# Router logits of an AdaLN attention and mixture-of-LoRA block computed with the router's weights held in the array, then transposed back

## What is computed

```python
h = layernorm(x) * (1 + ca) + sa
x = x + ga * attention(h)                      # causal, one head of 256, layer norm and residual inside
h = layernorm(x) * (1 + cb) + sb
x = x + gb * ffn(h)

def ffn(x):                                    # x flattened to rows of 256
    gate, up = x @ Wg.T, x @ Wu.T              # 704 hidden columns
    base = silu(gate) * up @ Wd.T
    probs = softmax(x @ Wr.T)                  # the router: 8 experts
    topw, topi = top_k(probs, 2)               # two experts for each row
    expert_w = sum(one_hot(topi, 8) * topw)
    for e in range(8):                         # LoRA of rank 16 for each expert
        g = x @ Ag[e].T @ Bg[e].T * 2;  u = x @ Au[e].T @ Bu[e].T * 2
        h = silu(gate + g) * (up + u)
        acc += (h @ Ad[e].T @ Bd[e].T * 2) * expert_w[:, e]
    return base + acc
```

## Time and profile before

| | |
|---|---|
| median of 3 runs | 670.26 us (670.22 to 670.79) |
| the profiled execution | 669.96 us, of which the span from first to last instruction is 668.1 us |
| granted TensorE clock, mean | 0.997 of full speed |
| PE busy | 652.1 us, 98% of the span, 3890 matmuls |
| DVE, ACT, POOL busy | 466.5, 360.3 and 369.5 us |
| DMA queue of the data | 6.6% of 16 engines' span |

### The profile page before, as it was taken

The page is one execution under the profiler, slowest core; times in us unless marked ns, Lnnn a source line. Parts: engine busy times, 40 slices in busy tenths (PEclk is TensorE's granted clock), DMA queues, the critical chain, the costliest instruction groups (busy, mean ns, idle before and its releaser), DMA issues.

```text
span 668.1 us, 10913 instructions
## 1 busy us (share of the span) xinstructions
PE 652.1 (98%) x3890; PEld 561.4 (84%) x3890; DVE 466.5 (70%) x1146; ACT 360.3 (54%) x646; POOL 369.5 (55%) x442
## 2 busy tenths in 40 slices
PE   8799999999999999999999999999999999999996
PEld 6488987888889987888889897887889998798885
DVE  5857676888785776688776677689886757547323
ACT  1766466545555547555455446564455456654543
POOL 1099366538658236657676317665666525633644
PEclk9999999999999999999999999999999999999999
DMA  8400020000000020000000001000000000000000
GB/s 308 138 1 1 2 64 0 1 1 32 0 1 32 1 65 1 0 1 33 0 1 32 1 6 59 1 1 33 1 0 27 7 1 1 1 1 1 32 0 33
DMA packets 15032, 15.47 MB, mean 23 GB/s; under 512 B 1793, under 2 KB 13697, under 8 KB 14977
## 3 DMA queue, kind: packets, MB, share of 16 engines
q1 hardware_dynamic: 14976, 14.76, 6.6%
HBM read 10.57 MB, written 4.19 MB: 22 GB/s over the span
## 4 chain that ended last, share of the span: by engine, by line
PE 84%; DVE 10%; ACT 3%; issue 1%; DMA 1%; POOL 0%; SPq 0%; DVEq 0%; ACTq 0%
PE ps L1265 78%; PE ps L1274 6%; DVE hid L1112 2%; DVE rstd L844 1%; DVE zb L864 1%; DMA xs<-in_L_attn_x 1%; DVE neg_mean L1176 1%; ACT xr L587 1%; ACT act_s L725 1%; DVE zb L867 0%; DVE stat L998 0%; DVE stat L861 0%; DVE topi L1057 0%; DVE xr L1007 0%; DVE nr_a L842 0%
## 5 line engine op out<-in xcount | busy, mean ns | idle before, releaser
L475 POOL TENSOR_TENSOR ring_lo<-hid,ring_hi 128x512 fp32r<-128x512 f32 x144 | 187.2, 1304 | 110.0 <-ACT ring_hi L733 109.4
L725 ACT ACTIVATE act_s<-ps 128x512 f32<-128x512 f32 x120 | 71.6, 597 | 123.0 <-PE ps L1265 122.4
L1112 DVE TENSOR_TENSOR hid<-act_s,ps 128x512 f32<-128x512 f32 x120 | 82.1, 684 | 78.9 <-ACT act_s L725 74.1
L733 ACT ACTIVATE ring_hi<-hid 128x512 fp32r<-128x512 f32 (+1 forms) x144 | 90.4, 627 | 5.3 <-PE ps L1265 3.5
L1265 PE MATMUL ps<-wdT_hi,ring_hi 128*128 128x256 f32 x192 | 53.2, 283 | 0.0
L1265 PE MATMUL ps<-wdT_lo,ring_hi 128*128 128x256 f32 x192 | 52.7, 280 | 0.0
L467 POOL TENSOR_TENSOR xT_lo<-tr_full,xT_hi 128x512 fp32r<-128x512 f32 x28 | 35.9, 1297 | 29.0 <-ACT xT_hi L597 29.0
L1265 PE MATMUL ps<-wdT_hi,ring_lo 128*128 128x256 f32 x160 | 44.7, 280 | 0.0
L1265 PE MATMUL ps<-vv_hi,pT_hi 128*128 128x256 f32 x144 | 42.9, 298 | 0.1
L1265 PE MATMUL ps<-tm_hi,bgT_hi 128*128 128x512 f32 x96 | 39.5, 411 | 2.4 <-DVE hid L1112 2.4
L482 POOL TENSOR_TENSOR xr<-xr,y_gb 128x256 f32<-128x256 f32 x31 | 22.6, 754 | 33.6 <-DVE y_gb L1147 33.6
(11 more groups left out here) (232 smaller groups left out, 2018.2 us busy)
## 6 DMA issues: line engine op xcount, KB each, us to landing
out<-xr SPq DMA_DIRECT2D x7, 512.0 KB, 2.9
xs<-in_L_attn_x SPq DMA_DIRECT2D x3, 1024.0 KB, 5.7
xs<-in_L_attn_x SPq DMA_DIRECT2D x2, 512.0 KB, 4.7
s_mod<-in_L_wmod SPq DMA_DIRECT2D x2, 512.0 KB, 7.6
s_qkvT<-in_L_attn_qkv SPq DMA_DIRECT2D x1, 768.0 KB, 7.4
wgT_raw<-in_L_ffn_Wg SPq DMA_DIRECT2D x1, 704.0 KB, 7.9
wuT_raw<-in_L_ffn_Wu SPq DMA_DIRECT2D x1, 640.0 KB, 8.7
wdT_raw<-in_L_ffn_Wd SPq DMA_DIRECT2D x1, 640.0 KB, 5.7
```

The lines of the kernel that those rows point to most:

```text
L475: pool.tensor_sub(ring[1][:, place(n), :], hid[:, n % HID, :], ring[0][:, place(n), :].bitcast(fp32)).then_inc(h_lo.sem, 1)
L725: nc.scalar.activation(act_s[:, n % 2, :], ps[:, 2 * (n % 2), :], ACT.Silu).then_inc(silu_ready.sem, 1)
L733: nc.scalar.activation(ring[0][p0:P, place(n), :], hid[p0:P, n % HID, :], ACT.Copy).then_inc(h_hi.sem, 1)
L1112: V.tensor_mul(hid[:, n % HID, :], act_s[:, n % 2, :], ps[:, 2 * (n % 2) + 1, :]).then_inc(h_ready.sem, 1)
```

## The change

`logits(ci)` is split in two. `logits_across(ci)` holds the router's weights in the array (16 or 8 columns) and moves all 512 rows of x past them: 2 k x 2 = 4 matmuls; the logits come out turned, 16 partitions by 512. A new DVE instruction, `logits_copy(ci)`, copies them out of PSUM into `logit_rows`, a view of 16 partitions of the tile `y_gb`. `logits_back(ci)` on PE waits for the copy and turns them back with 4 transposes, into the places where the logits stood before. DVE's `router_shift` waits for these. Two semaphores are new.

In half 0, `logits_across(0)` stands where `logits(0)` stood, and `logits_back(0)` behind the second piece of `probs_values`. In half 1, `logits_back(1)` stands one base product later, and `FILL` moves two `down`s behind the next `adapters`. On DVE, `router_shift(1)` moves behind the statistics of that step, and the moments and the guess of the next batch's first norm behind `hidden(13)`; POOL's three Newton steps for it come one unit later.

```diff
+        logit_rows = y_gb[0:2 * E, :, :].rearrange("p t d -> p (t d)")
...
-                            if not last and 13 <= r < 13 + NEWTON:
-                                newton(b, LN1_X, 0, NT, r - 13)
+                            if not last and 14 <= r < 14 + NEWTON:
+                                newton(b, LN1_X, 0, NT, r - 14)
...
+                def logits_copy(ci):
+                    dve.wait_ge(logits_wide.sem, logits_wide.at(b, ci))
+                    if ci == 0:
+                        dve.wait_ge(out_ready.sem, out_ready.at(b, -1))
+                    V.tensor_copy(logit_rows, ps[0:2 * E, LOGIT_BANK[ci], :]).then_inc(logits_copied.sem, 1)
...
+                logits_copy(0)
                 router_shift(0)
...
                     if r == 12:
-                        router_shift(1)
+                        logits_copy(1)
...
+                        if r == 13:
+                            moments(range(NT))
+                            guess(0, NT).then_inc(norm_ready.sem, 1)
...
-                        if r == 12:
-                            moments(range(NT))
-                            guess(0, NT).then_inc(norm_ready.sem, 1)
+                    if r == 12:
+                        router_shift(1)
...
-                def logits(ci):
+                def logits_across(ci):
 
                     pe.wait_ge(tr_lo.sem, tr_lo.at(b, KT * NC + ci * KT + 1))
+                    o = ps[0:2 * E, LOGIT_BANK[ci], :]
+                    for k in range(KT):
+                        x_hi, x_lo = inputs(ci)[k]
+                        mm(o, wr_both[:, k, :, :].rearrange("p h e -> p (h e)"), x_hi, k == 0, False)
+                        last_mm = mm(o[0:E, :], wr_both[:, k, 0, :], x_lo, False, k == KT - 1)
+                    last_mm.then_inc(logits_wide.sem, 1)
+
+                def logits_back(ci):
+
+                    pe.wait_ge(logits_copied.sem, logits_copied.at(b, ci))
                     for t in range(TC):
-                        o = ps[:, LOGIT_BANK[ci], 2 * t * E:2 * (t + 1) * E]
-                        for k in range(KT):
-                            x_hi, x_lo = [x_[:, t * P:(t + 1) * P] for x_ in inputs(ci)[k]]
-                            mm(o, x_hi, wr_both[:, k, :, :].rearrange("p h e -> p (h e)"), k == 0, False)
-                            last_mm = mm(o[:, 0:E], x_lo, wr_both[:, k, 0, :], False, k == KT - 1)
-                    last_mm.then_inc(logits_ready.sem, 1)
+                        last = transpose(ps[:, LOGIT_BANK[ci], 2 * t * E:2 * (t + 1) * E], logit_rows[:, t * P:(t + 1) * P], ident[0:2 * E, 0:2 * E])
+                    last.then_inc(logits_ready.sem, 1)
...
-                FILL = {(0, 0): (0, 0, 0, 0), (0, 1): (0, 1, 1, 1), (0, 2): (2, 2, 2, 1),
+                FILL = {(0, 0): (0, 0, 0, 0), (0, 1): (0, 1, 1, 1), (0, 2): (0, 4, 2, 1),
...
                         if ci == 0 and g == 2:
-                            logits(1)
+                            logits_across(1)
                         if g:
                             base(ci, g, 1)
+                        if ci == 0 and g == 2:
+                            logits_back(1)
...
-                logits(0)
+                logits_across(0)
                 probs_values(NT - 1, range(PV_FIRST, NT))
+                logits_back(0)
```

More of the change, by code:

```diff
@@ L240, in adaln_attention_moe_lora @@
         logits_ready = signal("logits_ready", NC)
+        logits_wide = signal("logits_wide", NC)
+        logits_copied = signal("logits_copied", NC)
         shifted_ready = signal("shifted_ready", NC)
```

## The result

The changed kernel takes 673.1 us, median of five runs (672.56 to 673.95). The kernel before, run beside it, takes 670.26 us (669.58 to 670.94). The ratio is 1.0043, with a 95% interval of 1.003 to 1.0056: slower by 2.8 us. The profiled execution took 673.1 us with a span of 671.3; the one of before had a span of 668.1. The mean granted clock is 0.996.

What follows compares the result with a forecast made beforehand. PE bounds the kernel, with DVE's router chain deciding half 0's masks. Half 0 +4.0 and half 1 -1.9 give +2.1 on 670.26, so 672.4 us; own range 671.9 to 673.3, overall range 671.0 to 674.8.

Steps and rivals of the forecast that it cites:

- Half 0 on PE: PE from half 0's router to the masks: 2.74 us instead of 3.20, so 0.46 earlier.
- Half 0, the chain: DVE's router chain up to half 0's masks starts and ends 0.99 us later; +4.0 (3.6 to 4.6) over four batches.
- The copy: DVE's logits copy in half 0: 0.65 to 0.76 us, hidden in DVE's idle 2.56, costs nothing itself.
- Half 1: PE's router in half 1: 1.33 us instead of 1.80, gain 0.47, four times -1.9 (1.6 to 2.0).
- Both covers: Half 1: PE reaches the transposes 0.1 to 0.2 us after the copy, the first down 0.4 after the shifted logits.
- The step that failed: POOL's Newton steps in half 1 go one unit later; no cost counted, as POOL idles there (55% busy).
- A: Half 1's gain is lost too through thin covers: +4.0 up to +5.0, 674.3 to 675.3; 14%.
- B: Half 0's added latency doesn't reach the masks, both halves gain: 3.7 us faster, 666.5; 6%.
- C: Router matmuls with narrow stationary operands step faster than 0.23, at 0.11: -1.8, 668.5; 4%.
- The estimate from the Trainium skill: 131 ns per 512-column matmul: half 0's four router matmuls take 0.52 us, sum about -1.1, 669.2.
- D: PE's wait of 0.59 some 17 us behind half 0's masks absorbs part of the added 1.0: -0.3, 670.0; 7%.

Runs made afterwards that it cites:

- fill_undone: The changed kernel with the old FILL numbers, the two downs back ahead of the adapters in half 1: 678.1 us, ratio 1.0114 to the kernel before.
- newton_in_idle: Kernel before with half 1 changed, one x1_stats moved behind the last xr product, POOL's Newton steps behind half 0's last low part: 667.43 us, ratio 0.9952.
- half0_only: Kernel before with only half 0's router changed (across, copy, back), half 1 as before: 674.62 us against 670.57, ratio 1.0064.
- steps_moved: newton_in_idle with one of DVE's second-norm Newton steps in half 0 moved behind the next hidden block: 666.45 us, ratio 0.9937 to the kernel before.

## Why the prediction was right, and where it was not

The forecast was +2.1 us (672.4), the measurement +2.8 (673.1): the sign, the mechanism and the size hold, inside the case's own range of +1.6 to +3.0. Point by point:

1. **Half 0 on PE.** Four matmuls across at 0.23 each, 0.92: as expected. The twelve of the second piece start over 1.29 us and would be 1.41 with one more step of 0.12, as argued, but the transposes start 0.21 behind the last of them (82.00, 82.21), so there is 0.09 that I had not counted: my sum had an extra only behind the transposes, and there is one on either side. The four transposes took 0.35 for the expected 0.33, and the matmul behind them stepped by 0.33, an extra of 0.10 for the expected 0.08. From the router's first matmul to the last one ahead of the masks PE takes 6.75 where it took 7.12: it is 0.37 earlier, not 0.46.

2. **Half 0, the chain.** DVE's first router copy at +2.87 was predicted and measured at 2.87, though two errors cancel in it: the transposes came 0.09 later, and from the first transpose's start to DVE's start it took 0.45 instead of 0.54. Masks at 8.55 were expected, 8.55 to 8.57 measured; +4.0 in both. That the sum comes out to the hundredth is luck in this one place; the chain itself is the same 5.14 from DVE's start to the last `xr` product (82.66 to 87.80). The kernel with half 0 alone gives +4.05 by its medians, and the one with earlier transposes shows that the masks follow the chain's start at 1:1.

3. **The copy.** 0.68 us is inside the bounds of 0.65 to 0.76. It lay in DVE's idle time and did not delay PE. Put into the chain it cost 0.59 per batch; its place decides.

4. **Half 1.** Both covers held, 0.3 us at the transposes and 0.5 at the first down (expected 0.1 to 0.2, and 0.4). The term itself is right for a partly wrong reason. By the PE rows, the router with the transposes and what they add to the steps on either side costs 1.49 where it cost 1.81, a gain of 0.32 and not 0.47: the same uncounted extra ahead of the transposes, 0.09, and some 0.05 in them and behind them. The stretch is 0.55 shorter nonetheless, since the 48 matmuls of the `down`s that now stand in one row, 121.78 to 127.22, step by 0.113 us, where the 24 behind 119.14 and the 24 behind the next adapters stepped by 0.118: 5.44 us for 5.66. Half 1 is 23.89 in each of the five other kernels of the experiments that have the new form and the new table. In fill_undone, with the same new router but the `down`s in two rows of 24, the second row steps by 0.118 again, so it goes with the one long row and not with the router. Why the longer row steps faster I don't know. In sum -2.2 for -1.9. The router alone would have given four times 0.32, -1.3, outside the -1.6 to -2.0 of the prediction, so it is luck that the term comes out near it.

5. **The step that failed** is the sentence that POOL's Newton steps come one unit later and cost nothing because POOL idles there, 55% busy. I read an average over the span at a place where POOL was not idle: before the change it had 0.2 to 0.7 us of slack there. The cost is 0.17 per batch in three batches of the changed kernel, 0.5 us; in the kernel that newton_in_idle started from it was 0.26, 0.8 us. By stages the account is +4.0 - 2.2 + 0.5, and 0.3 for the longer wait at the end, which the forecast did not have either and whose cause is open: +2.6. The 0.2 between that and the medians' +2.8 is no larger than the spread of the runs. The `down`s' faster step, which nobody foresaw, offsets most of what was missed.

6. **The rivals.** A (half 1's gain is lost): no, half 1 alone is -1.44 and its stretch 0.55 shorter; its mechanism is real, though, since fill_undone shows it at 1.3 us per batch. B (the latency doesn't reach the masks): no, it reaches them whole. C (narrow stationary operands step faster): no, 0.22 to 0.24 in the rows above. The estimate from the Trainium skill, "TensorE: Matmul & The Clock Gate", section "Back-to-back issue gap", would put the four at 0.52 us; the rows say 0.92, so for this stream the measurement decides. D (the wait of 0.59 absorbs part): no, it is the same 0.59 in half0_only.

The change thus cuts PE's work in both halves, by 0.37 us in half 0 and 0.32 in half 1, where the `down`s' step adds 0.22. In half 1 PE was the limit and it counts. In half 0 a chain through DVE was the limit, and the change lengthened that chain by a round trip. The better kernel takes the new form in half 1 alone.

## What to carry to other kernels

An exchange of many short matmuls for few long ones plus a copy and transposes saves time on PE and adds a round trip to the first consumer. Look at each place of use whether PE or the consumer's chain arrives last at the next meeting point, and take the new form only where it is PE. When a step moves to a "free" engine or a later slot, read that engine's rows in that slot: a busy share of 55% over the span said nothing about the unit in which POOL had 0.2 us left.

## What the runs showed of the hardware

**A copy of 16 partitions takes as long on DVE as an instruction of 128.** The copy of 16 partitions by 512 takes 0.67 to 0.68 us, and an instruction of 128 partitions by 512 that reads PSUM takes 0.69 (the hidden block above).

**A narrow stationary operand does not speed up a matmul.** With 16 or 8 columns and 512 moving, the step is 0.22 to 0.24 us, as with 128 columns.

**A small DVE instruction can be held until a POOL one ends.** Two DVE rows of newton_in_idle, the same operation once ahead of and once under a `ring_lo` of POOL:

```profile
257.31 0.16 DVE L848 SCALAR_TENSOR_TENSOR rstd<-nr_a,rstd 128x4 f32<-128x4 f32 x1
...
257.90 1.15 DVE L848 SCALAR_TENSOR_TENSOR rstd<-nr_a,rstd 128x4 f32<-128x4 f32 x1
259.08 0.69 DVE L1122 TENSOR_TENSOR hid<-act_s,ps 128x512 f32<-128x512 f32 x1
```

and POOL's row beside them:

```profile
257.74 1.28 POOL L478 TENSOR_TENSOR ring_lo<-hid,ring_hi 128x512 fp32r<-128x512 f32 x1 [1.44 <-ACT ring_hi L737]
```

The operation of 0.16 us lasts 1.15 when it starts 0.16 behind POOL's, and ends at 259.05, when POOL ends at 259.02. The hidden block behind it (259.08) is the one for which PE waits 0.59. What it reads from ACT was ready at 257.15, so as far as the trace shows it starts about a microsecond later than it could have. This agrees with the Trainium skill, "SBUF — State Buffer", section "SBUF: two separate sides": DVE and GpSimd share a pair of ports under an exclusive lock, and whoever starts first holds it for the whole instruction. The operation has two operands in SBUF, as the Trainium skill asks for where POOL reads SBUF too; `ring_lo` reads both of its operands there. It is not a single case: in the kernel before, 9 of DVE's 134 instructions with an operand of 128x4 last over 0.4 us. All nine start while an instruction of POOL runs and end 0.02 to 0.03 behind it; five of them are a `TENSOR_SCALAR`. A `TENSOR_REDUCE` (`lmax<-lg`) under a `ring_lo` is not held: 0.19, four times. In steps_moved an operation of DVE is held in the same way by the same `ring_lo` (0.95 us, but behind the hidden block, which starts ahead of that `ring_lo`). No kernel here was built to keep the two engines apart, so what that would be worth stays open.
